# DMA instead of TensorE for turning the attention weights in 24 more windows, and a new order of the first loads

## The reference, cut to what matters

```python
# x, ctx: [8, 512, 2048] f32; H = 8 heads of d = 256; topk = int(2 * log(512)) = 12
def autocorrelation(Q, K, V):             # Q = layernorm(x), K = V = ctx
    corr = ifft(fft(q, axis=time) * conj(fft(k, axis=time))).real
    w, idx = top_k(corr over the 512 lags, per head and channel)
    w = softmax(w)
    out = sum_i w[i] * v[min(idx[i] + pos, L - 1)]      # v shifted by each kept lag
x = x + autocorrelation(layernorm(x), ctx, ctx)
# second half: a linear layer with 16 low-rank experts, folded into one weight matrix
h = layernorm(x)
x = x + h @ W.T + bias + sum_e coeffs[e] * scales[e] * (h @ A[e].T) @ Bf[e].T
```

## Time and profile before

| | |
|---|---|
| Median of 3 runs | 2739.56 us (2738.73 to 2742.19) |
| Profiled execution, its own time | 2732.36 us |
| Its span, first to last instruction | 2730.2 us |
| PE busy | 2622.6 us, 96% of the span |
| POOL, DVE, ACT busy | 2157.0, 1812.5, 1065.3 us |
| Time of DMA packets, share of 16 engines' span (queue q1) | 70.4% |
| Mean granted clock of TensorE | 0.988 of full speed |

### The profile page before, as it was taken

The page is one execution under the profiler, slowest core; times in us unless marked ns, Lnnn a source line. Parts: engine busy times, 40 slices in busy tenths (PEclk is TensorE's granted clock), DMA queues, the critical chain, the costliest instruction groups (busy, mean ns, idle before and its releaser), DMA issues.

```text
span 2730.2 us, 39047 instructions
## 1 busy us (share of the span) xinstructions
PE 2622.6 (96%) x13792; PEld 1684.0 (62%) x13792; DVE 1812.5 (66%) x4710; ACT 1065.3 (39%) x1837; POOL 2157.0 (79%) x1558
## 2 busy tenths in 40 slices
PE   4999967899999999999999999999999999999998
PEld 3666655566666666666666666666666666654444
DVE  5888879667776677667776677667765677644100
ACT  4787746433354244433353235433342234201000
POOL 5799999779887889888887789888888789655222
PEclk8999988999999999999999999999999999999999
DMA  8499998955685666856685576855685576648953
GB/s 317 104 262 267 261 244 188 267 177 208 228 252 183 205 235 235 251 177 214 227 253 187 191 254 236 235 189 205 226 225 160 185 252 228 178 163 305 295 169 116
DMA packets 486675, 597.74 MB, mean 219 GB/s; under 512 B 259280, under 2 KB 385360, under 8 KB 468816
## 3 DMA queue, kind: packets, MB, share of 16 engines
q1 hardware_dynamic: 486480, 595.25, 70.4%
HBM read 383.35 MB, written 151.00 MB: 196 GB/s over the span
## 4 chain that ended last, share of the span: by engine, by line
PE 80%; POOL 7%; DMA 5%; DVE 4%; SPq 2%; issue 1%; ACT 1%; POOLq 0%; DVEq 0%; ACTq 0%
PE f_ps L814 15%; PE f_ps L816 15%; PE f_ps L818 15%; PE a_ps L698 10%; PE a_ps L740 10%; PE a_ps L779 7%; PE a_ps L795 3%; PE a_ps L794 3%; POOL p_lo L1173 1%; DMA p_hi_t<-p_hi 1%; PE a_ps L753 1%; SPq L535 1%; DMA x_scratch<-a_rows 1%; DMA p_w<-in_L_ffn_W_dram 1%; DMA p_lo_t<-p_lo 1%
## 5 line engine op out<-in xcount | busy, mean ns | idle before, releaser
L814 PE MATMUL f_ps<-f_whi,f_hhi 128*128 128x512 f16 x2048 | 776.2, 379 | 2.1 <-DMA f_hlo<-h_scratch 1.8
L818 PE MATMUL f_ps<-f_whi,f_hlo 128*128 128x512 f16 x2048 | 776.2, 379 | 0.0
L816 PE MATMUL f_ps<-f_wlo,f_hhi 128*128 128x512 f16 x2048 | 776.2, 379 | 0.0
L898 ACT ACTIVATE a_side<-a_ps 128x256 f32<-128x256 f32 (+1 forms) x192 | 87.1, 454 | 1031.5 <-PE a_ps L779 798.5
L740 PE MATMUL a_ps<-a_w_lag,lags 128*128 128x256 f16 x3072 | 356.7, 273 | 1.0 <-DVE a_tf L1207 1.0
L818 PEld LDWEIGHTS f_ps<-f_whi,f_hlo 128*128 128x128 f16 x2048 | 200.4, 98 | 241.7
L816 PEld LDWEIGHTS f_ps<-f_wlo,f_hhi 128*128 128x128 f16 x2048 | 200.4, 98 | 226.7
L740 PEld LDWEIGHTS a_ps<-a_w_lag,lags 128*128 128x128 f16 x3072 | 300.8, 98 | 60.2 <-issue 4.8
L814 PEld LDWEIGHTS f_ps<-f_whi,f_hhi 128*128 128x128 f16 x2048 | 200.4, 98 | 212.3 <-issue 2.5
L1080 POOL TENSOR_TENSOR a_prod<-a_prod,a_tf 128x512 f32<-128x512 f32 x128 | 160.4, 1275 | 187.0 <-DVE a_tf L1207 187.0
L1080 POOL TENSOR_TENSOR a_zv<-a_zv,a_tw 128x512 f32<-128x512 f32 x128 | 183.1, 1449 | 128.9 <-DVE a_tf L1207 128.9
(11 more groups left out here) (132 smaller groups left out, 5153.2 us busy)
## 6 DMA issues: line engine op xcount, KB each, us to landing
f_whi<-whi_scratch SPq DMA_DIRECT2D x128, 512.0 KB, 5.5
f_wlo<-wlo_scratch SPq DMA_DIRECT2D x128, 512.0 KB, 6.6
a_rows<-in_x_dram SPq DMA_DIRECT2D x62, 1024.0 KB, 8.4
vs<-in_ctx_dram SPq DMA_DIRECT2D x64, 512.0 KB, 7.6
xs<-in_x_dram SPq DMA_DIRECT2D x64, 512.0 KB, 3.7
parts_scratch<-a_so SPq DMA_DIRECT2D x64, 512.0 KB, 4.8
x_scratch<-a_rows SPq DMA_DIRECT2D x32, 1024.0 KB, 5.1
f_x1p<-x_scratch SPq DMA_DIRECT2D x32, 1024.0 KB, 6.2
```

What stands on the lines that cost most here:

```text
L814: nc.tensor.matmul(f_ps[:, t, :], h_hi[q][:, kq, rows_t], w_hi[u % WR][:, :, kq, :], start=(k == 0), stop=False)
L816: nc.tensor.matmul(f_ps[:, t, :], h_hi[q][:, kq, rows_t], w_lo[u % WR][:, :, kq, :], start=False, stop=False)
L818: mm = nc.tensor.matmul(f_ps[:, t, :], h_lo[q][:, kq, rows_t], w_hi[u % WR][:, :, kq, :], start=False, stop=(k == DB - 1))
L898: return nc.scalar.activation(out, source, ACT.Copy, **how)
```

## The change

Three edits. `turned_by_dma` takes in windows i = 3 to 6, 24 chunks more (four for each of the first six batch rows). SP loads all four first tiles of x ahead of the values of chunk 0. ACT makes one tiny copy first, which brings the load of its function table ahead, and normalises the queries of chunk 0 before it moves the values; DVE waits for that copy before its first statistics.

```diff
@@ turned_by_dma(n)
-            return n < N and at is not None and at[1] < 3
+            return n < N and at is not None and at[1] < 7
@@ sync
             load_first_rows(0, rows[0][:, :])
             load_first_rows(1, rows[1][:, :])
-            shared.load_v(sp, 0)
             load_first_rows(2, w_sb[:, 0, :])
             load_first_rows(3, w_sb[:, 1, :])
+            shared.load_v(sp, 0)
             shared.load_x(sp, 0)
@@ scalar
             act.wait_ge(mask_set, 2)
+            copy(f_shift[:, :], rows_but_0[:, :]).then_inc(table_loaded, 1)
             double_last(0)
+            act.wait_ge(x_link, LINKS + 2)
+            normalise(0)
             move_values(0)
             move_upper(0)
-            act.wait_ge(x_link, LINKS + 2)
-            normalise(0)
             double_last(1)
@@ vector
+            dve.wait_ge(table_loaded, 1)
             for k, source in enumerate((rows[0][:, :], rows[1][:, :], w_sb[:, 0, :], w_sb[:, 1, :])):
                 first_statistics(k, source)
```

More of the change, by code:

```diff
@@ L300, in flow @@
         mask_set = sem("a_mask_set")
+        table_loaded = sem("a_table_loaded")
         q_normed = sem("a_q_normed")
```

## The result

The changed kernel takes 2780.72 us (median of 6 runs, 2775.24 to 2788.80), the kernel before 2739.14 beside it: ratio 1.0153, 95% interval [1.0135, 1.0171]. It is slower, by less than forecast. The profiled execution took 2782.06 us, with a span of 2780.3; its own time is 49.7 us more than that of the profiled execution before, where the prediction had 58. The medians are 41.6 us apart.

A forecast was written before the change was run, and what follows sets the result against it. PE, busy 96% of the span, was taken as the bound. Per batch row, stalls 10.4 plus clock 3.6 less 4 x 0.89 gave 10.4 us; six made 62, less 4 at the start: +58, 2798 us, range 2756 to 2845.

The forecast's parts named there:

- The 0.89 us a window: Windows i = 3 to 6: PE work saved per window by dropping its 16 transposes, 21.4 us over 24 windows.
- the small stalls: Rival: turning costs 2.2 us, POOL catches up more, no clock loss in i = 3 to 6; +22, 2762 us; chance 0.16.
- I take 2.6: Windows i = 3 to 6: second turning lands 2.6 us behind the transfer ahead, plus 0.1 until PE starts.
- The lower end: Smallest delay of the second turning behind the transfer ahead, 2.2 us, read from window 14's similar outstanding transfers.
- The burst moves ahead by 0.8 in i = 4 and 1.4 in i = 6: POOL catches up while PE stalls, so transfers ahead of the turning come 0.8 and 1.4 us sooner.
- 1.8 each, 3.6 a batch row: PE work lost to a lower clock after the stalls in i = 4 and 5: 1.8 us each.
- -4 at the start: The new load and ACT order start correlate(0) 4 us sooner, near 37.5 us; bounds 0 to 5.
- ACT normalises them soon after the statistics, while the values are folded: At the start, queries no longer wait behind the moved values; a step towards the 4 us gain.
- I let the 4 us through to the end: Later windows follow the first, so the start's whole 4 us gain was counted in the total.
- The turning hides after all: Rival: PE gets turned weights in time in all 24 windows; -25 us, 2714 us; chance 0.12.
- SP held at the issue: Rival: turning lands 3.5 us behind the transfer ahead, clock lost in all four windows; +109, 2849 us; chance 0.12.
- No change: Rival: losses of 1.1 us a window pay back both gains, no measurable change; chance 0.04.

The follow-up runs named there:

- the four places of the turning: The changed kernel with its DMA turning behind the row tile's store, ahead of the values, unmoved, or behind the partial sums' store: 2712.41, 2751.18, 2780.72, 2816.62 us.

## Why the prediction was right, and where its sizes were off

**The direction and its reason held.** The turning is gated by the transfer issued ahead of it, not by its own length. That was read from the time that this transfer lands and from window 14, and the four places of the turning confirm it. The 0.89 us a window was exact. Luck has a share in how near the number came: without window 28's 13.5 us, which no term of the sum stood for, the spans would lie 36.6 us apart, 21 below the forecast's 58 and 15 above the 22 of the small stalls.

**"I take 2.6."** The second turning landed 1.9 to 2.0 us behind the transfer ahead, in window 26 of three kernels the same to 0.1, and 1.8 to 1.9 in most windows of the changed kernel. The lower end, 2.2 from window 14, was the nearer row; I had weighed it with a pile-up that didn't come. SP was indeed held at the issue (8.38 us for two, against 2.99 in window 14), but the landing didn't wait for that. 0.6 us too much in each of 24 windows is 14 us, about the whole difference in stalls, 62.4 against 47.4, though not window by window: i = 5 came out 0.8 over, since its last row landed later than in the trace before and three of its turnings came 2.4 to 2.6 behind it.

**"The burst moves ahead by 0.8 in i = 4 and 1.4 in i = 6."** The mechanism is right, the sizes were not constants. By the issue of the row tile's store, counted from `correlate`: in i = 6 it moved from 15.5 us to 13.3 in four windows, by 2.2. In i = 4 it stood at 14.2 before and depended on whether i = 3 had stalled: 13.3 where it had by 1.5 us or more, 0.9 sooner, and 14.5 where it hadn't, 0.3 later than before. Hence stalls in i = 4 of 2.2 to 2.4 us in three batch rows and of 3.6 to 4.7 in the others, where I had 4.1 throughout.

**"1.8 each, 3.6 a batch row" for the clock.** 21.6 forecast, 7.6 measured. The windows view (its columns as in the earlier trace rows) of the stretch behind the stall of window 26, and of the one after it:

```profile
1007.80:1010.90 3.10, 3.06 (x15) 2.21 (x16) 0.23 (x1) 0.00 (x0) 0.00 (x0) 0.50 1.08 296
1010.90:1014.70 3.80, 3.80 (x25) 2.26 (x24) 2.35 (x4) 0.00 (x0) 1.19 (x1) 1.00 0.93 307
```

3.1 us at the 1.2 GHz level, 1.5 us lost, then full clock again: less than the 4.2 us stretch of the earlier trace rows had made me think. And most stalls cost no clock: in this trace four of 19. Over the eight profiled executions with a late turning, the granted clock fell behind 1 of 69 stalls shorter than 2.25 us, behind 31 of 62 from there to 3.85, and behind 27 of 28 longer ones, for 1.3 to 2.9 us each. I had charged every stall in i = 4 and 5. In this the rival of small stalls was the nearer, and its 2.2 for the turning too; its 4.4 us a batch row lacks window 28, which is 2.3 a batch row by itself.

**"-4 at the start."** 1.7 us at `correlate(0)`. The step that failed is "ACT normalises them soon after the statistics, while the values are folded": I put statistics and fold side by side as if they didn't touch, and the statistics took 3.9 us more for it, as POOL waiting for them showed. Whether "I let the 4 us through to the end" failed too isn't shown: 0.1 is left at `correlate(14)` in one execution, within a scatter of 4 us, and the start by itself was 3.3 us faster in the medians (0.8 to 5.7 by the interval). From `correlate(63)` to the end the changed kernel took 3.1 us more; the other twelve profiled executions, with this same code, lie between 326.0 and 330.8 us there (before 326.2, changed 329.3), so nothing is read into it.

**The sum on the profiled execution:** stalls 47.4, clock 7.6, window 28 13.5, transposes -21.4, start -0.1, end +3.1: 50.1, the difference of the spans. The prediction's 58 had two terms too large (stalls by 15, clock by 14), one missing (13.5), one gain too large (3.9) and the end at nothing (3.1), so part of it met by errors that cancel. The rest of the distance to 2798 is that I set the median 7.2 us above the profiled execution, where it lay 1.3 below it.

**The rivals.** *The turning hides after all* needed the turnings to land ahead of what was issued before them: in none of the 19 windows that have both landings did they. In the whole trace of the changed kernel 4 of 1070 transfers landed ahead of one issued before them, by less than 1 us. *SP held at the issue* is right that SP is held and wrong on what it does to the landing. *No change* is out.

**What stays open:** why DVE gets its turn after one or two of POOL's operations nearly wherever the two meet (row pieces of 2.4 to 4.7 us up to `correlate(63)`) and in two of the profiled executions not for ten. Both times it had started 0.06 us behind the start of a 0.7 us add; two cases show a pattern and no mechanism, and no run set this distance on purpose. That fewer adds of POOL in a row would prevent it wasn't tried.

## What to carry to other kernels

Before a DMA takes over work from a full engine, read where it stands in its queue: add issue and time to landing of the transfer ahead of it, and compare with the time at which the consumer wants the data. Here the same two DMAs were worth -22 us at the head of a burst (2712.41 against 2734.01 with the new start alone) and +40 at its end (2777.52 against 2737.26), and what they were moved ahead of had the slack. Where DVE and POOL both work on SBUF, an operation that is moved to run beside the other engine's isn't free, and a short one can cost many times its length; look for the same line at two durations before and after.

## What the runs showed of the hardware

- Two transposing DMAs issued into a full queue landed 1.0 and 1.9 us behind the transfer ahead of them, whatever stood further ahead (window 26 of three kernels: 1.01 and 1.92, 1.04 and 1.97, 0.96 and 1.88). Three windows of 19 in the changed kernel had 2.4 to 2.6 for the second.
- SP was held 8.38 us by these two issues in a full queue, against 2.99 in window 14, and up to 5.54 us by one.
- A DVE operation with two SBUF inputs took 17.74 us in place of 2.28 beside ten of POOL's adds back to back, in two executions, each time started 0.06 us behind the start of a short add. Started 0.17 us ahead of POOL's adds it took 2.28, and they 4.47 in place of 2.48. In the first chunks of the run, where the same subtraction reads one input from PSUM, it took 2.27 us with POOL's adds beside it at full speed.
- Four of the six operations on 128x4 elements that ran beside POOL's 1.27 us adds took 1.1 to 1.2 us, the other two 0.16 and 0.17, as all do without the adds; one of the slow four has a single SBUF tensor as its input.
